# A fused attention and expert block: two kinds of heads in one attention unit, transposed probabilities of two units in one buffer, and two copies that move from VectorE to ScalarE

## The reference

```
xn  = layernorm(x)
q,k,v = heads(xn @ W + b)                    # 16 heads of 8 features
s   = (q @ k.T + q . rel_k[clip(j - i, -20, 20)]) / sqrt(8)
p   = softmax(s)                             # 16 x 16 x 512 x 512
w   = p @ v + sum_j p[i,j] * rel_v[clip(j - i, -20, 20)]
out = x + w @ Wo.T + bo + ffn(xn)            # ffn: 4-head attention, then 8 experts, top 2
```

## Time and profile before

| | us |
|---|---|
| median of 3 runs | 2552.55 (2547.36 to 2559.85) |
| the profiled execution | 2548.51, span 2546.7 |
| `attend`, from first to last score matmul | 282.0 to 1629.5 |
| busy over the span: PE, DVE, ACT, POOL | 2238.3, 1974.6, 1578.1, 976.6 |

### The profile page before, as it was taken

The page is one execution under the profiler, slowest core; times in us unless marked ns, Lnnn a source line. Parts: engine busy times, 40 slices in busy tenths (PEclk is TensorE's granted clock), DMA queues, the critical chain, the costliest instruction groups (busy, mean ns, idle before and its releaser), DMA issues. The chain is left out here.

```text
span 2546.7 us, 77672 instructions
## 1 busy us (share of the span) xinstructions
PE 2238.3 (88%) x27816; PEld 1550.5 (61%) x27816; DVE 1974.6 (78%) x4345; ACT 1578.1 (62%) x3954; POOL 976.6 (38%) x1190
## 2 busy tenths in 40 slices
PE   5673599999999999999999999779999996999999
PEld 3442366666666666666666666546656664666665
DVE  5663499888988899988998999647776764787777
ACT  4442377777777777877777778547767762222222
POOL 5764245444544555454535554300000002333332
PEclk9886699999999999999999999879999997999999
DMA  6987245444554455545455554300101001101010
GB/s 191 275 260 216 79 106 124 112 107 109 124 112 113 111 123 114 114 114 122 111 116 113 120 116 91 62 23 26 37 25 37 25 30 63 30 29 33 25 37 17
DMA packets 568040, 241.18 MB, mean 95 GB/s; under 512 B 462279, under 2 KB 531655, under 8 KB 563143
## 3 DMA queue, kind: packets, MB, share of 16 engines
q1 hardware_dynamic: 567750, 237.26, 37.4%
HBM read 133.87 MB, written 103.29 MB: 93 GB/s over the span
## 5 line engine op out<-in xcount | busy, mean ns | idle before, releaser
L896 ACT ACTIVATE a_probs<-a_bank_s,a_neg_max 128x512 f32<-128x512 f32 x1024 | 693.6, 683 | 195.4 <-DVE a_neg_max L823 188.3
L823 DVE TENSOR_REDUCE a_neg_max<-a_bank_s 128x2 f32<-128x1024 f32 x512 | 627.0, 1225 | 55.3 <-DVE a_bank_s L793 1.4
L676 PE MATMUL a_bank_pt<-a_ident,a_probs 128*128 128x128 f32 x4096 | 570.8, 282 | 30.2 <-ACT a_feat_t L908 29.9
L676 PEld LDWEIGHTS a_bank_pt<-a_ident,a_probs 128*128 128x128 f32 x4096 | 443.2, 142 | 146.8 <-issue 67.2
L876 ACT ACTIVATE a_probs_t<-a_bank_pt 128x512 f32<-128x512 f32 x512 | 305.1, 596 | 162.4 <-PE a_bank_pt L676 161.1
L809 DVE COPY a_probs_t<-a_bank_pt 128x512 f32<-128x512 f32 x512 | 349.9, 683 | 34.2 <-PE a_bank_pt L676 33.8
L665 PE MATMUL a_bank_s<-a_k,a_q 48*32 48x512 bf16 (+15 forms) x4096 | 270.9, 287 | 67.5 <-DMA a_kl<-scr_parts 63.9
L695 PE MATMUL a_bank_o<-a_probs_t,a_v 128*32 128x128 f32 x8192 | 281.3, 279 | 0.0
L665 PE MATMUL a_bank_s<-a_kl,a_q 48*32 48x204 bf16 (+14 forms) x3840 | 241.8, 266 | 31.0 <-ACT a_probs L896 25.1
L1560 ACT ACTIVATE e_gate<-e_bank_g 128x512 f32<-128x512 f32 x144 | 86.0, 597 | 275.8 <-PE e_bank_g L1499 275.8
L695 PEld LDWEIGHTS a_bank_o<-a_probs_t,a_v 128*32 128x32 f32 x8192 | 211.6, 111 | 55.7 <-ACT a_probs_t L876 41.0
(11 more groups left out here) (166 smaller groups left out, 3645.6 us busy)
## 6 DMA issues: line engine op xcount, KB each, us to landing
scr_probs<-a_probs SPq DMA_DIRECT2D x256, 144.0 KB, 4.5
a_raw<-scr_qr SPq DMA_DIRECT2D x256, 96.0 KB, 2.9
scr_qr<-p_qr SPq DMA_DIRECT2D x64, 320.0 KB, 3.1
a_feat<-scr_probs SPq DMA_DIRECT2D x256, 78.0 KB, 2.4
scr_parts<-p_sp SPq DMA_DIRECT2D x144, 128.0 KB, 3.0
a_left<-scr_probs SPq DMA_DIRECT2D x256, 64.0 KB, 2.4
a_q<-scr_parts SPq DMA_DIRECT2D x32, 192.0 KB
a_k<-scr_parts SPq DMA_DIRECT2D x32, 192.0 KB
```

The source lines that it names most:

```text
L676: ins = nc.tensor.transpose(b_pt[bank_of(job)][:, 0, t * P:(t + 1) * P], probs[(u - 1) % 4][:, j, MAX_REL + t * P:MAX_REL + (t + 1) * P], ...
L823: nc.vector.tensor_reduce(neg_max[:, 2 * pair:2 * pair + 2], b_s[:, 2 * pair:2 * pair + 2, :], AX.X, ALU.max, negate=True).then_inc(max_ok, 1)
L896: nc.scalar.activation(probs[u % 4][:, j, MAX_REL:MAX_REL + S], b_s[:, j, :], ACT.Exp, bias=neg_max[:, j:j + 1], accum_out=sums[:, t, j, u ...
```

## The change

- Heads: blocks 0 and 1 of a unit keep head index u % 4, blocks 2 and 3 take `u % 4 ^ 1` (`head_of`). The array rows of a matmul follow the parity of the head, so a unit uses both halves of the rows.
- Order of blocks: `PLACES = (0, 2, 1, 3)`; the first pair of a unit now holds blocks 0 and 2, the second 1 and 3, so each pair has one block of either parity. `scores` issues the KL matmuls of both blocks and then the K matmuls of both.
- `probs_t` holds two units (`2 * NQB` tiles), `spot` puts a tile so that `attended` can take one head of both units; `attended` runs one unit later (u-3) and waits for copies in every second unit only.
- Copies: in units with u % 4 == 2 tile 3 is copied by ScalarE, behind the unit's last exponential, and no more by VectorE; `last_t` is copied by ScalarE behind `feat_t`. The `o_sb` copy of ScalarE goes from unit 1 to unit 2.
- SP stores a unit's probabilities with two DMAs in place of one. GpSimd makes `moved_wide` with three operations in place of one.

```diff
+PLACES = (0, 2, 1, 3)
+def head_of(u, i):
+    return u % 4 ^ i // 2
+def spot(u, i):
+    return (2 * (u % 2) + i) if i < 2 else (6 - 2 * (u % 2) + i - 2)
...
-        probs_t = [sb(f"probs_t{s}", [P, NQB, S]) for s in range(2)]
+        probs_t = [sb(f"probs_t{s}", [P, 2 * NQB, S]) for s in range(2)]
...
-                par = slice((u % 2) * HALF, (u % 2) * HALF + ROWS)
-                for i in pair:
-                    at = u // 4 * P + i * QBLK
-                    edge = max(at - MAX_REL, 0)
-                    for keys, a, z in ((KL, 0, edge), (K, edge, S)):
+                for right in range(2):
+                    for p in pair:
+                        i = PLACES[p]
+                        at = u // 4 * P + i * QBLK
+                        edge = max(at - MAX_REL, 0)
+                        keys, a, z = (K, edge, S) if right else (KL, 0, edge)
                         if a == z:
                             continue
+                        par = head_of(u, i) % 2 * HALF
...
-                after = (b, u + 1) if u < UNITS - 1 else (b + 1, 0)
-                for j in (2, 3):
-                    job_read(pe, after[0], (after[1], "probs", j))
+                after = (b, u + 2) if u < UNITS - 2 else (b + 1, 0)
+                if u % 2 == 0:
+                    for j in range(4):
+                        job_read(pe, after[0], (after[1], "probs", j))
...
-                            if u > 1 and not tail:
-                                attended(b, u - 2, s)
+                            if u > 2 and not tail:
+                                attended(b, u - 3, s)
...
 (VectorE)
-                        if (u and not tail) or (u == 0 and not first):
+                        if ((u and not tail) or (u == 0 and not first)) and not (u % 4 == 2 and pair):
                             read_probs(b, u, 2 * pair + 1)
...
-                        nc.vector.tensor_copy(last_t[:, t], b_pt[bank_of(job)][:, 0, 0:P]).then_inc(pt_ev[bank_of(job)], 1)
...
 (ScalarE)
-                    if u == 1 and not first:
+                    if u % 4 == 2 and not tail:
+                        read_probs(b, u, 3)
+                    if u == 2 and not first:
                         act.wait_ge(av_ps, b * UNITS)
...
+                        job = (u, "features", 1)
+                        job_done(act, b, job)
+                        nc.scalar.activation(last_t[:, (u // 4 - 2) % NT], b_pt[bank_of(job)][:, 0, 0:P], ACT.Copy
+                                             ).then_inc(pt_ev[bank_of(job)], 1)
```

More of the change, by code:

```diff
@@ L746, in row @@
                         if pair[0]:
-                            if u > 1 and not tail:
-                                attended(b, u - 2, s)
+                            if u > 2 and not tail:
+                                attended(b, u - 3, s)
                                 if first and u == 3:
                                     warm_up(nc, b_w[:, 0, 0:P], ident[:], WARM)
-                            elif u < 2 and not first:
-                                attended(b - 1, u + UNITS - 2, 1 - s)
+                            elif u < 3 and not first:
+                                attended(b - 1, u + UNITS - 3, 1 - s)
                         for j in pair:
@@ L784, in add_window @@
             def add_window(u, pair):
-                t, hh = u // 4, u % 4
+                t = u // 4
                 first, last = t == 0 and pair == 0, t == NT - 1 and pair == 1
-                for i, n in ((0, 1), (1, 1)) if first or last else ((0, 2),):
-                    i += 2 * pair
+                for k, n in ((0, 1), (1, 1)) if first or last else ((0, 2),):
+                    p = 2 * pair + k
+                    i = PLACES[p]
                     edge = t * P + i * QBLK - MAX_REL
                     a, z = max(edge, 0), min(edge + WIN, S)
-                    whole = b_s[:, i, a:z]
-                    near = bass.AP(whole.tensor, whole.offset, [whole.ap[0], [S + QBLK, n], [1, z - a]])
-                    ins = nc.vector.tensor_tensor(near, near, win[t % 2][:, i:i + n, hh, a - edge:z - edge], ALU.add)
+                    whole, own = b_s[:, p, a:z], win[t % 2][:, i, head_of(u, i), a - edge:z - edge]
+                    near = bass.AP(whole.tensor, whole.offset, [whole.ap[0], [S + 2 * QBLK, n], [1, z - a]])
+                    step = (2 * NJ + head_of(u, 2) - head_of(u, 0)) * WIN
+                    ins = nc.vector.tensor_tensor(near, near, bass.AP(own.tensor, own.offset, [own.ap[0], [step, n], [1, z - a]]),
+                                                  ALU.add)
                 return ins
@@ L952, in make_feature @@
                                         ones[:], ALU.mult).then_inc(wide_ok, 1)
[L953 to L954 removed]
+                for i, units, heads in ((0, slice(0, 4), slice(0, 4)), (2, slice(0, 4, 2), slice(1, 4, 2)),
+                                        (2, slice(1, 4, 2), slice(0, 4, 2))):
+                    out = moved_wide[:].rearrange("p (i h) d -> p i h d", i=NQB)[:, i:i + 2, heads]
+                    far = left_less_right[:].rearrange("p (i h) d -> p i h d", i=NQB)[:, i:i + 2, heads]
+                    n = 4 if i == 0 else 2
+                    ins = nc.gpsimd.tensor_tensor(out, moved[:, t, i:i + 2, units].rearrange("p i (h o) -> p i h o", o=1)
+                                                  .to_broadcast([P, 2, n, HD]), far, ALU.mult)
+                ins.then_inc(wide_ok, 1)
                 g.wait_ge(l_in, b * 64 * NT + 64 * (t + 1))
```

44 lines of the change are left out of this document (22 added, 22 removed).

## The result

The changed kernel takes 2653.73 us (median of 4 runs, 2649.0 to 2661.63), the kernel before 2550.57 us. The ratio is 1.0381, 95% interval 1.0345 to 1.0417: 103 us slower. The forecast was 2571, the range ended at 2612. Every kernel further down was timed next to runs of the kernel before, whose medians were 2554.4, 2552.0 and 2552.8 us in the three groups; so a difference of a few us between kernels of different groups says nothing, and the ratio is what to compare.

What follows compares the result with a forecast made beforehand. The prediction took a chain changing engine, 20.58 us per four units, as the bound. +27 us for 64 groups and -9 us at unit 6 made +18 on 2548.5: 2567, or 2571 on the median's scale; range 2538 to 2612.

Steps and rivals of the forecast that it cites:

- Scores in two halves: Score matmuls of a pair run side by side in the array: 0.55 us becomes about 0.35, saving 0.20.
- The first rival: Score matmuls in bf16 are not parallel in two halves and gain nothing: +38 us, 2609; chance 0.12.
- the stall: PE's new wait before tile 1's transposes in every fourth unit, for ScalarE's tile 3 copy; some 1.6 us.
- the legs: Four parts of the pace-setting chain over four units, before the change 7.97, 7.18, 1.65 and 3.78 us, together 20.58.
- legs 1 and 2: Unit 12's second reduce to unit 14's scores, 0.20 us shorter; from there to VectorE's add, 7.18 becoming 7.69.
- leg 3: VectorE's add to its copy, where PE's scores, attended and transposes come late: 1.65 us becoming 1.77, +0.12.
- The wait of PE and its direct price: PE waits for ScalarE's late tile 3 copy; with shorter scores, +0.43 us per four units, +27 us in 64 groups.
- `last_t` worth 0: Moving this copy to ScalarE frees VectorE, but its later copy still waits on the feature copy: 0 us.
- Unit 6: VectorE's sum, once a row, costing 0.60 us, falls into its idle time before tile 1: -9 us over 15 rows.
- the change does what it says: Rival: tile 3's bank is free before PE wants it, saving 1.2 us a group, -77 us, 2476; chance 0.10.
- the clock is at its upper level: Starting assumption from the profile of `attend`: PE runs at full clock, 2.4 GHz in the score estimate.
- The queue of SP: 256 more issues, counted 0; as a rival, up to 0.8 us late at 15 row starts, 2583, chance 0.10.

Runs made afterwards that it cites:

- early loads: The next row's loads issued one place earlier; on the changed kernel with tile 3 back on VectorE 2515.8 us, without them 2542.4 us.
- idle products: Changed kernel plus matmuls whose result nobody reads, in TensorE's wait between the transposes of tiles 0 and 1: six 2581.4 us, three 2581.5 us.

## Why the prediction was wrong

- *Scores in two halves: right.* A pair takes 0.34 us (1189.13 to 1189.47, forecast 0.35), both KL groups of a pair in one row of eight. The first rival, that bf16 would gain nothing, is refuted. What it is worth on the chain was put too high for a kernel without the stall. With tile 3 on VectorE and early loads the legs are 7.76, 7.00, 1.59 and 3.77 us: legs 1 and 2 lose 0.21 and 0.18, leg 3 only 0.06, since 1.59 is what VectorE's own add and reduce take. In the sum with the stall TensorE is late in leg 3 and the 0.20 counts.
- *The wait of PE and its direct price: right.* 1.53 us before the transposes of tile 1 (forecast "some 1.6 us"), legs 7.76, 7.66 and 1.77. A clean row with the stall (idle products, no low clock in it) is 84.7 us against 83.4: 1.3 us in 16 rows, 21 us. The sum said 18.
- *`last_t` worth 0: right for the chain* (equal clean rows); a difference of 9 to 11 us elsewhere is not clear of noise and stays open.
- *Unit 6: right.* With the copy on VectorE unit 6 takes 4.90, in the changed kernel 4.44, while unit 10 goes from 4.30 to 4.44: 0.60 less, as forecast.
- *The rival "the change does what it says"* (2476) was not what happened, and its price was too high as well. With ScalarE's copy ahead of the exponentials and early loads the bank is free in time, and the legs are 7.76, 6.59, 1.98 and 3.78: 0.47 us a group less than before, where the rival had 1.2. Leg 2 lost 0.59 and not 0.80, and leg 3 grew by 0.33. That kernel takes 2513.2.
- *The step that failed* is in the first paragraph: "the clock is at its upper level". Every duration of the sum was taken at that level and kept there, and no rival had the clock. The prediction saw the wait of 1.5 us itself and priced only its place in the chain. In the change the clock falls to the lower level 61 times, not 6; with the late copy alone it is 24 times, with the rest of the change alone 13, so most of the 61 need both. The changed kernel is at the lower level for 188 us more than before, at 0.45 us each: 85 us. 21 + 85 = 106, measured 103. The idle products, which leave the late copy where it is, gave back 72 us (171 us of low clock less; times 0.45 is 77).
- *The queue of SP, counted 0:* too low for the kernels with fewer stalls, where early loads are worth 24 to 27 us. In the changed kernel it was worth nothing measurable: 1.3 us of waits for these loads in the window.

The Trainium skill, TensorE: Matmul & The Clock Gate, section A second HAM failure mode: psum-queue depth-cycling, describes a kernel in which short waits of TensorE between groups of matmuls make the clock go back and forth between its two levels. The trace here agrees: 61 stretches at 0.5 with full clock between them. Had that rule stood among the rivals, the price of a stretch could have been read from the lower-clock stretches of the kernel before; how many the change would add could not.

## What to carry to other kernels

A wait that costs 0.4 us a group on the chain cost four times as much here with the clock. Shorter work on TensorE did little to the clock alone (13 low stretches against 6), but with it the same late copy brought 61 low stretches in place of 24. So price each new gap twice, once on the chain and once by the stretch at the lower level that may follow. A copy moved to another engine goes where its bank is next wanted; here ahead of two exponentials instead of behind them was worth 110 us. When an engine frees time in every unit, look at what was just in time before: the last load of the next row, here some 24 us.

## What the runs showed of the hardware

A stretch of 3.70 us with one wait of 1.50 us, in which TensorE was busy 2.21 us, was followed by 3.4 us at 1.2 GHz, in which 32 fp32 matmuls took 1.93 us instead of 1.08. Each such stretch made its row about 1.5 us longer. Three idle products of 128 columns in that wait, which leave 0.87 us empty, cut the stretches from 61 to 17; six cut them to 12. And bf16 matmuls of 48 rows in the two halves of the array, into different banks, ran side by side: the 1024 columns of a pair, on four column groups, in 0.34 us instead of 0.55.
